# Palette weights as outer products of hat values on TensorE, two tile lags longer, and a new order of the pieces

## The chip, the cores and the metric

The kernel runs on one NeuronCore of a Trainium2 chip. The metric is the device time of one execution in microseconds, median of the runs. Five engines work from instruction streams of their own and meet only at semaphores: TensorE (PE, its weight loads are shown as PEld), VectorE (DVE), ScalarE (ACT), GpSimd (POOL) and SyncE (SP, which issues DMAs).

## The reference, cut to what matters

Eight residual layers follow each other over 2,048 tokens of 128 features: a recurrent attention with a clipped 8x8 state, a mixture of experts (first kind), the palette layer, the same mixture again, linear attention, a mixture of experts (second kind), a decayed recurrent attention, and the second mixture again. The change is at the palette layer. For each token it picks 15 earlier tokens, runs a small network over their relations, and gets for each pick k a point (gx, gy) and a mixing weight. It then reads a 16x16 picture (the palette, 128 channels) at the 15 points by bilinear interpolation and sums:

```
z = jnp.tanh(h @ Wc + bc)
w = jnp.nan_to_num(jax.nn.softmax(mix, axis=-1))
fx = jnp.clip((gx + 1.0) * 0.5 * (PW - 1), 0.0, PW - 1)
fy = jnp.clip((gy + 1.0) * 0.5 * (PH - 1), 0.0, PH - 1)
...
samples = ((1 - wy) * (1 - wx))[..., None] * g(y0, x0) + ((1 - wy) * wx)[..., None] * g(y0, x1) + ...
V = jnp.einsum('btkd,btk->btd', samples, w[:, 0])
y = jnp.einsum('btd,dm->btm', V, Wo[0])
```

The four bilinear factors are products of two "hats", relu(1 - |fx - x|) over the 16 columns x and relu(1 - |fy - y|) over the 16 rows y. So each token needs a 16x16 matrix of weights, the sum over k of w_k hat(fy_k, y) hat(fx_k, x), and then a product of these 256 weights with palette times Wo.

## The kernel before, in words

The tokens are 16 tiles of 128. Twelve stages pass over them, each written as a generator that yields between pieces: `front` (f), `gram` (g) and `scan` (s) with `out` (o) are the first attention, `ffn2` (a) and `ffn4` (b) the first mixture, `pal` (p) and `mix` (m) the palette layer, `lin` (l) linear attention, `ffn6` (c) and `ffn8` (e) the second mixture, `dec` (d) the decayed attention. For each engine a string, `ORDER`, says stage by stage by one letter whose next piece comes; the instructions of an engine stand in that order and are executed in it. Tiles of different stages so overlap like a pipeline. The scan of the first attention is a strict chain over the 2,048 tokens in pairs (64 steps a tile on DVE: L916 product, L924 scan), helped by small matmuls on PE, L539 and L549.

`ffn2` and `ffn4` share buffers and one count of uses; `LAG = 2` says by how many tiles the uses of `ffn4` stand behind those of `ffn2`. `ffn6` and `ffn8` share likewise, and alternate without a lag (uses 2c and 2c + 1).

The piece in question, `mix`, goes for a tile like this. After the small network (PE L674 to L696), DVE adds a bias, ACT takes tanh and exp, DVE scales and clips the coordinates (L1123, L1126) and makes the weights (L1129, L1131). POOL subtracts the grid (L1693, 30 x 16 values per token), ACT makes |.| and relu (L1462, L1465), and POOL multiplies the y hats by the weights (L1698). Then 8 times: POOL makes the products of the hats of two picks with tokens on partitions (`pr`, 128x512, L1705), and PE transposes and sums them in PSUM by matmuls with `pr` as weights and the identity as moving operand (L704, four or two of 128x128, each of two passes as all f32 matmuls here). ACT copies the sum (L1469), two matmuls multiply it by `palWo` (L712, L713) and DVE adds it to the residual (L855).

Each layer norm has on DVE statistics (L841, L843), the addition of eps (L845) and the normalisation (L849), and between the last two a power on POOL (L1573).

Of the kernel before, what the change touches and what calls it, by code (L numbers as in the profile page):

```python
# [99 lines left out]
LN_V, LN_G, LN_A, LN_P = ["bs", "ba", "le", "xn"], ["lr"], ["xt"], ["T"]  # L100
# [8 lines left out]
        "ssfffggffgsgsfssgsfsfsgsssssssgssssssssgssssssfssgsossosoosofssfsgsosossasaasssgsasaasasasassspgspsssspsfspp"  # L109
        "ppsosgsoososossssgsssosossasaasssasaasasasasfgsfmsgpmsspmsmssmmpsfmpspmmmsompmgpsoosoomsmssmsmsgsososmmsmsam"  # L110
        "saassgsasaasmsasaasmsmfsmmspfsmspmsmgsmmmsmmbspbbsfosmpmpmsmmmmpmobobbspoobbbsgmsmlslmsmsgsssllollllsomsmmms"
        "slslsacsacsamccsmccccsmccamsaascmasaasdmdspfsmdddspmgmfddddbsmgbbesmsefsmeebseeebebeebbebsomspolsolsmosospsm"
        "pmmllllllsmmsmpmgpgfsfllsmsmcsmcsomoccmccccmccsmsamsaacssadaadsadddaammddsmsgddsmmspgespmesmseeeeeeeesmsfesm"
        "smmsombmbbsosoospobmmmsmbbpspmbbbsmmopmgsopfllsamsaasllllllsmsamgssaamlsalsamasmmsmcgcfsccccccsccsmcsmsmdspm"
        "dsmdddsmpmgmsddmddsmsmbmebbsfesmeeboeeebebesebbebsoosolsposmmmlspspmsmmmpmsgllllllsmmpgsomomlsfmlsmmsmfcsscs"
        "gccsmccccccsasmcsaasmmsdmdsadddsaammmmsddddsaasamesgmebsbbeespeeeeeespfbebbsombbbsoosolsolsmspgsllllllspmsmp"
# [1862 lines left out]
```

## Time and profile before

| | |
|---|---|
| median of 3 runs | 1754.71 us (1746.64 to 1755.44) |
| profiled execution | 1746.41 us, span 1744.3 us |
| granted TensorE clock, mean | 0.768 |
| busy: PE, DVE, POOL, ACT | 1376.0, 1242.0, 969.9, 702.4 us |
| HBM traffic | 15 GB/s over the span |

The span is from the first to the last instruction. Busy time of an engine is the time in which at least one of its instructions is shown as running. Granted clock 1.0 is 2.4 GHz, 0.5 is 1.2 GHz; there is nothing between them in this trace, so a mean of 0.768 is a mixture.

### The profile page before, as it was taken

The numbers are of one execution on the slowest core, as the hardware profiler recorded it, in microseconds if no ns is written. First come the engines' busy times: TensorE is split into PE (matmuls) and PEld (weight loads), VectorE is DVE, ScalarE is ACT, GpSimd is POOL, SyncE is SP. The second block draws the span as 40 slices with busy tenths as digits, with TensorE's granted clock in tenths as the row PEclk, the third lists the DMA queues.
The fourth block names the chain that finished last, engine by engine and source line by source line (L and its number), as shares of the span: only waits on it lengthen the run. The fifth ranks groups of instructions, "written<-read, shape, count | busy, mean of one in ns | idle before, by whom it ended". The sixth has DMA issues, their size and how long they took to land.

```text
span 1744.3 us, 42130 instructions
## 1 busy us (share of the span) xinstructions
PE 1376.0 (79%) x15708; PEld 951.5 (55%) x15708; DVE 1242.0 (71%) x5282; ACT 702.4 (40%) x1833; POOL 969.9 (56%) x1423
## 2 busy tenths in 40 slices
PE   2576887788988888788888898988889787867764
PEld 0233464556665655656575665656465655646543
DVE  3878778877877776778777788787778874534432
ACT  1222545453545445344526353553515243424221
POOL 2337667557575654766574757474564636362421
PEclk9555778888788688878878697768869686868865
DMA  5001000000000100000000100010010100000000
GB/s 139 1 1 29 19 13 24 6 19 14 12 21 5 27 3 19 15 18 11 19 14 5 27 5 26 6 27 3 4 27 5 27 5 22 10 20 6 1 2 4
DMA packets 24007, 28.93 MB, mean 17 GB/s; under 512 B 8953, under 2 KB 18842, under 8 KB 23794
## 3 DMA queue, kind: packets, MB, share of 16 engines
q0 software_dynamic: 8208, 16.57, 3.6%
q1 hardware_dynamic: 15586, 9.57, 1.9%
q8 instruction: 128, 2.10, 0.5%
q14 instruction: 85, 0.70, 0.1%
HBM read 24.71 MB, written 2.23 MB: 15 GB/s over the span
## 4 chain that ended last, share of the span: by engine, by line
PE 50%; DVE 28%; POOL 7%; ACT 7%; issue 6%; SPq 1%; DMA 0%; DVEq 0%; ACTq 0%; POOLq 0%
PE ps L704 5%; PE ps L626 4%; DVE sb L1187 4%; DVE ps L924 4%; PE ps L674 2%; PE ps L525 2%; DVE ps L916 2%; PE ps L651 2%; PE ps L767 2%; PE ps L806 2%; PE ps L760 2%; PE ps L539 2%; POOL sb L1684 2%; PE ps L607 2%; PE ps L814 2%
## 5 line engine op out<-in xcount | busy, mean ns | idle before, releaser
L924 DVE TENSOR_TENSOR_SCAN ps<-ps,sb 128x47 f32<-128x47 f32 (+3 forms) x1024 | 271.5, 265 | 35.1 <-DVE ps L916 0.5
L1684 POOL DMA_INDIRECT sb<-table,sb x240 | 235.9, 983 | 78.4 <-issue 54.5
L916 DVE TENSOR_TENSOR ps<-sb,ps 128x24 f32<-128x24 f32 (+3 forms) x1024 | 193.0, 188 | 13.2
L1573 POOL TENSOR_TENSOR sb<-sb 128x1 f32<-128x1 f32 x128 | 72.1, 563 | 169.3 <-DVE sb L845 168.6
L704 PE MATMUL ps<-sb 128*128 128x128 f32 x960 | 161.4, 322 | 2.1 <-POOL sb L1705 2.0
L1705 POOL TENSOR_TENSOR sb<-sb 128x512 f32<-128x512 f32 (+1 forms) x128 | 128.4, 1009 | 42.9 <-PE ps L704 41.2
L704 PEld LDWEIGHTS ps<-sb 128*128 128x128 f32 x960 | 142.3, 227 | 8.6 <-issue 3.2
L1250 ACT ACTIVATE sb<-ps 128x128 f32<-128x128 f32 x128 | 35.0, 276 | 212.2 <-PE ps L497 211.6
L855 DVE TENSOR_TENSOR sb<-ps,sb 128x128 f32<-128x128 f32 x128 | 36.8, 288 | 115.1 <-PE ps L781 59.4
L549 PEld LDWEIGHTS ps<-sb 32*32 32x32 f32 x2032 | 45.4, 116 | 119.2 <-issue 92.5
L539 PEld LDWEIGHTS ps<-sb 32*32 32x32 f32 x2032 | 44.2, 118 | 112.2 <-DVE sb L896 66.1
L539 PE MATMUL ps<-sb 32*32 32x32 f32 x2032 | 75.1, 223 | 33.8 <-DVE sb L896 33.0
L549 PE MATMUL ps<-sb 32*32 32x12 f32 x2032 | 68.1, 196 | 40.3 <-DVE sb L932 36.9
L525 PE MATMUL ps<-sb 128*128 128x480 f32 x128 | 87.3, 775 | 7.7 <-POOL sb L1594 2.4
L626 PE MATMUL ps<-sb 128*128 128x128 f32 x512 | 85.4, 325 | 0.0
L497 PE MATMUL ps<-sb 128*128 128x128 f32 x128 | 45.6, 360 | 49.7 <-DVE sb L849 46.4
L1165 DVE TENSOR_TENSOR sb<-sb,ps 128x512 f32<-128x512 f32 (+1 forms) x96 | 61.2, 640 | 28.3 <-ACT sb L1516 15.3
L1594 POOL TENSOR_TENSOR sb<-sb 128x480 f32<-128x480 f32 x64 | 64.7, 1022 | 27.1 <-ACT sb L1289 27.0
L626 PEld LDWEIGHTS ps<-sb 128*128 128x128 f32 x512 | 78.8, 237 | 0.7
L1439 ACT ACTIVATE sb<-ps 128x512 f32<-128x512 f32 x64 | 64.3, 1041 | 30.4 <-PE ps L663 30.4
L849 DVE TENSOR_SCALAR sb<-sb 128x128 f32<-128x128 f32 x128 | 58.1, 454 | 23.1 <-POOL sb L1573 22.7
L1756 POOL TENSOR_TENSOR sb<-sb 128x128 f32<-128x128 f32 x32 | 12.9, 403 | 110.8 <-ACT sb L1523 110.7
(300 smaller groups left out, 3725.8 us busy)
## 6 DMA issues: line engine op xcount, KB each, us to landing
sb<-table,sb POOLq DMA_INDIRECT x240
sb<-in_cs SPq DMA_DIRECT2D x16, 128.0 KB
sb<-in_x SPq DMA_DIRECT2D x4, 256.0 KB, 9.5
table<-sb SPq DMA_DIRECT2D x16, 64.0 KB, 1.8
sb<-dscr SPq DMA_DIRECT2D x64, 2.0 KB
out<-sb SPq DMA_DIRECT2D x16, 64.0 KB, 1.5
sb<-in_wex SPq DMA_DIRECT2D x1, 512.0 KB, 5.5
sb<-in_rvx SPq DMA_DIRECT2D x1, 512.0 KB, 4.6
```

Of the source, the lines that this page charges most:

```text
L525: e.matmul(b[:, 0:32 * LW], blk, g_.pp[j % 2][:, :], start=True, stop=True).then_inc(*g_.P("s"))
L539: x = e.matmul(psS[rows, 0:32], KZT[c % 2][rows, 32 * o1:32 * o1 + 32], R[g % 2][rows, :], start=g == 0, stop=True, skip_group_check=True)
L549: x = e.matmul(b[rows, 0:12], SB[g % 2][rows, :], KM[c2 % 2][rows, 4 * o2:4 * o2 + 4, :].rearrange("p a b -> p (a b)"), start=True, stop=True)
L626: x = e.matmul(b[:, 0:128], s.hw[j // 4][:, 128 * (j % 4):128 * (j % 4) + 128], wex[:, 128 * j:128 * j + 128], start=False, stop=j == 7)
L704: x = e.matmul(pb[:, 128 * h:128 * h + 128], p_.pr[k % 2][:, 256 * j + 128 * h:256 * j + 128 * h + 128], ident, start=(k == 0 and j == 0 a ...
L916: e.tensor_tensor(at(psP, p + ROW - 3 - 2 * m, [ROW, 3], [2, m], [1, 2]), AC[:, row(n, k), :, HIST - 2 * m:HIST].rearrange("p r (a b) -> p ...
L924: e.tensor_tensor_scan(at(psD, 16 + k + COMB * skip, [COMB, 3 * ROW - skip]), at(psP, p + skip, [1, 3 * ROW - skip]), Q[:, i % 32, skip:3 ...
L1187: e.tensor_tensor_scan(d_.pv[h][:, at], l[:, 128:256], d_.pv[h][:, at], cp[:, k:k + 1] if c % NT else 0.0, ALU.mult, ALU.add).then_inc(*d_ ...
L1573: e.tensor_tensor(st[:, 9:10], st[:, 8:9], mhalf[:, 0:1], ALU.pow).then_inc(*s.G("lr"))
L1594: e.tensor_tensor(g_.pp[j % 2][:, :].rearrange("p (a b c) -> p a b c", b=2, c=LW), at(KT[c % 3], 32 * j, [2, 16], [0, 2], [1, LW]), km[:, ...
L1684: e.indirect_dma_start(GA[:, k, :], None, table[0:128 * i + 129, :], bass.IndirectOffsetOnAxis(u[:, k:k + 1], 0)).then_inc(*p_.gat("gat"))
L1705: e.tensor_tensor(p_.pr[k % 2][:, 0:256 * m].rearrange("p (k y x) -> p k y x", y=16, x=16), hats[:, 1, 2 * k:2 * k + m, :].unsqueeze(3).to ...
```

## The change

For the palette's weights the products of hats move from POOL to PE. The coordinates and exponentials are transposed in 32x32 blocks on DVE (`e.transpose`), so that picks lie on partitions 32q to 32q + 14 for the 32 tokens of block q, 16 hat values to a token lie in a row. One matmul for each token then gives its 16x16 matrix: the y hats of 15 picks as weights, the x hats moving, 15 rows deep. Four such (q = 0 to 3) use four different 32x32 parts of the array; there are 32 x 4 of them for a tile. The product with `palW` becomes 16 x 4 matmuls of 16 rows and 128 moving columns. The softmax's division moves to the final addition. `H1` and `H2` of the small network now lie in the buffer `PT`.

Further: eps, the q/k norm arithmetic of `front` and two small maxima move from DVE to POOL; negations on DVE are folded into ACT and into the reduction; `sT`, `one8` and `selb` are padded with zeros from 24 to 128 rows, so that the matmuls L616 and L767 use all rows; `LAG` goes from 2 to 3, and `ffn8` gets a lag of 1 behind `ffn6` (`LAG1 = 1`); the strings of `ORDER` are new for all five engines.

```diff
-LAG = 2
+LAG = 3
+LAG1 = 1
...
-LN_V, LN_G, LN_A, LN_P = ["bs", "ba", "le", "xn"], ["lr"], ["xt"], ["T"]
+LN_V, LN_G, LN_A, LN_P = ["bs", "ba", "xn"], ["le", "lr"], ["xt"], ["T"]
...
 ORDER = {
     "PE":
...
-        "mmmmllcmcmmccmccccmccmmcmmddbdddbbddddbbbebebbeeeeeeeellellllllllcccccccccccdddddddddeeeeeeeeeee",
+        "ccccceeddeeddeeedeeeeddddeeeeeeeeeee",
...
-    selb, one8, identb = sb([24, HU], BF16), sb([24, 8], BF16), sb([128, 128], BF16)
+    selb, one8, identb = sb([128, HU], BF16), sb([128, 8], BF16), sb([128, 128], BF16)
...
@@ PE, ffn0 @@
-                        x = e.matmul(b[:, 128 * j:128 * j + 128], one8[:, 4 * h + j:4 * h + j + 1].to_broadcast([24, 128]),
+                        x = e.matmul(b[:, 128 * j:128 * j + 128], one8[:, 4 * h + j:4 * h + j + 1].to_broadcast([128, 128]),
@@ PE, mix @@
-            for k in range(8):
-                yield
-                w.wait_ge(*m_.V.at("z", c))
-                w.wait_ge(*m_.G.at(f"pr{k}", c))
-                for h in range(2):
-                    for j in range(2 if k < 7 else 1):
-                        x = e.matmul(pb[:, 128 * h:128 * h + 128],
-                                     p_.pr[k % 2][:, 256 * j + 128 * h:256 * j + 128 * h + 128], ident,
-                                     start=(k == 0 and j == 0 and h == 0), stop=(2 * k + j == 14), skip_group_check=True)
-                x.then_inc(*m_.P(f"acc{k}"))
...
-            e.matmul(b[:, 0:128], p_.c[:, 0:128], palWo[:, 0:128], start=True, stop=False)
-            e.matmul(b[:, 0:128], p_.c[:, 128:256], palWo[:, 128:256], start=False, stop=True).then_inc(*m_.P("mm"))
+            for k in range(32):
+                if k % 4 == 0:
+                    yield
+                    w.wait_ge(*m_.G.at("u4", c))
+                for q in range(4):
+                    rows = slice(32 * q, 32 * q + 15)
+                    x = e.matmul(pb[32 * q:32 * q + 32, 16 * k:16 * k + 16], hats[rows, 512 + 16 * k:544 + 16 * k],
+                                 hats[rows, 16 * k:16 * k + 16], start=True, stop=True)
+            x.then_inc(*m_.P("op"))
+            for k in range(16):
+                if k % 4 == 0:
+                    yield
...
+                for q in range(4):
+                    rows = slice(32 * q, 32 * q + 16)
+                    x = e.matmul(b[32 * q:32 * q + 32, 0:128], WT[rows, k:512:16], palW[rows, 128 * k:128 * k + 128],
+                                 start=k == 0, stop=k == 15)
+            x.then_inc(*m_.P("mm"))
@@ DVE, norm and mix @@
-            w.wait_ge(*s.V.at("ba", c))
-            e.tensor_scalar(st[:, 8:9], st[:, 7:8], 1e-5, None, ALU.add).then_inc(*s.V("le"))
...
-            e.tensor_scalar(t[:, 112:142].rearrange("p (j k) -> p k j", j=2), z3[:, :, 0:2], 7.5, 7.5, ALU.mult,
-                            ALU.add).then_inc(*m_.V("f1"))
-            w.wait_ge(*m_.V.at("f1", c))
-            e.tensor_scalar(t[:, 112:142], t[:, 112:142], 15.0, 0.0, ALU.min, ALU.max).then_inc(*m_.V("f2"))
+            e.transpose(crdT[:, 0:64], crd[:, 0:64]).then_inc(*m_.V("xy"))
             yield
             w.wait_ge(*m_.A.at("ex", c))
+            e.transpose(crdT[:, 64:96], crd[:, 64:96]).then_inc(*m_.V("wt"))
...
-            e.tensor_scalar(t[:, 96:111], t[:, 66:81], t[:, 83:84], None, ALU.mult).then_inc(*m_.V("wk"))
-            yield from add(m_, m_.P.at("mm", c), ("pal", "mm", c), c, i)
+            e.scalar_tensor_tensor(out=X[:, i, :], in0=bk.of["pal", "mm", c][:, 0:128], scalar=t[:, 83:84], in1=X[:, i, :],
+                                   op0=ALU.mult, op1=ALU.add).then_inc(*m_.X("x"))
@@ ACT, mix @@
-            e.activation(hs, hs, ACT.Abs).then_inc(*m_.A("ab"))
+            e.activation(hats[:, 0:1024], hats[:, 0:1024], ACT.Abs, scale=7.5).then_inc(*m_.A("ab"))
...
-            e.activation(p_.c[:, :], pb[:, 0:256], ACT.Copy).then_inc(*m_.A("c"))
+            e.activation(WT[:, :], pb[:, :], ACT.Copy).then_inc(*m_.A("c"))
@@ POOL, norm and mix @@
+            w.wait_ge(*s.V.at("ba", c))
+            e.tensor_scalar(st[:, 8:9], st[:, 7:8], 1e-5, None, ALU.add).then_inc(*s.G("le"))
...
-                e.tensor_tensor(p_.pr[k % 2][:, 0:256 * m].rearrange("p (k y x) -> p k y x", y=16, x=16),
-                                hats[:, 1, 2 * k:2 * k + m, :].unsqueeze(3).to_broadcast([128, m, 16, 16]),
-                                hats[:, 0, 2 * k:2 * k + m, :].unsqueeze(2).to_broadcast([128, m, 16, 16]),
-                                ALU.mult).then_inc(*m_.G(f"pr{k}"))
+            hy = hats[:, 512:1024].rearrange("p (t y) -> p t y", y=16)
+            e.tensor_tensor(hy, hy, crdT[:, 64:96].unsqueeze(2).to_broadcast([128, 32, 16]), ALU.mult).then_inc(*m_.G("u4"))
```

Two places of PE's order show what the new strings do. The first is in the middle of the program, before the change: the last of the palette weights of one tile, L704, between pieces of `scan` (L549) and of a mixture of the second kind (L591 to L767).

```order
L704 MATMUL ps<-sb 128x128 x4
L549 MATMUL ps<-sb 32x12 x4
L704 MATMUL ps<-sb 128x128 x4
L591 MATMUL ps<-sb 24x128
L760 MATMUL ps<-sb 128x128 x4
L704 MATMUL ps<-sb 128x128 x2
L767 MATMUL ps<-sb 128x128 x4
L760 MATMUL ps<-sb 128x128 x4
L767 MATMUL ps<-sb 128x128 x4
```

The end of the same work of a tile after the change: L708 are the outer products, L720 the product with `palW`; L551 is the former L549, L541 the former L539, L823 the former L814, L619 the former L616, L787 to L790 the end of a mixture of the second kind (before: L778 to L781), L594 the former L591.

```order
L551 MATMUL ps<-sb 32x12 x4
L708 MATMUL ps<-sb 32x16 x64
L594 MATMUL ps<-sb 24x128
L619 MATMUL ps<-sb 128x128 x4
L787 MATMUL ps<-sb 128x128
L788 MATMUL ps<-sb 128x128
L790 MATMUL ps<-sb 128x128 x11
L619 MATMUL ps<-sb 128x128 x4
L823 MATMUL ps<-sb 128x128 x2
L541 MATMUL ps<-sb 32x32 x4
L823 MATMUL ps<-sb 128x128 x2
L720 MATMUL ps<-sb 32x128 x16
```

What moved: 30 matmuls of a full array in eight pieces have become 128 small ones in up to eight pieces and 64 small ones in up to four. (In such rows a count is of matmuls; in the trace each f32 matmul is two instructions.)

The second place is the end of the program before the change, the last tile's `dec` (L794 to L814) and the start of its `ffn8`.

```order
L796 MATMUL ps<-sb 32x128
L800 MATMUL ps<-sb 128x128
L806 MATMUL ps<-sb 128x128 x8
L814 MATMUL ps<-sb 128x128 x8
L497 MATMUL ps<-sb 128x128
L752 MATMUL ps<-sb 128x8
L591 MATMUL ps<-sb 24x128
L760 MATMUL ps<-sb 128x128 x4
```

And after it, the last tile's `dec` (L805, L809, L815) with what now stands between, the `ffn8` of the tile ahead of it (L594, L769, L776).

```order
L805 MATMUL ps<-sb 32x128
L594 MATMUL ps<-sb 24x128
L769 MATMUL ps<-sb 128x128 x4
L809 MATMUL ps<-sb 128x128
L815 MATMUL ps<-sb 128x128 x4
L776 MATMUL ps<-sb 128x128 x4
L769 MATMUL ps<-sb 128x128 x4
L776 MATMUL ps<-sb 128x128 x4
L815 MATMUL ps<-sb 128x128 x4
```

What moved: `ffn8` of a tile stands one tile later. Counted over PE's strings, what comes after the last piece of the scan was 3 tiles of `ffn4`, 4 of `lin`, `ffn6`, `dec` and `ffn8` each, and 2.7 of `mix`; it is now 4.1, 5, 5, 5, 6 and 2.9 tiles. At the end of the fifth tile of the scan, one tile of `lin`, `ffn6` and `dec` was done; now none is. Counted over the same rows, PE changes between different shapes of the array's part in use (all 128 x 128, or 32 rows, or 32 columns, or both) 1,488 times before and 1,301 times now.

## Rows read from the trace of the kernel before

**Rows 1.** The page's parts 1 and 4: busy time, chain by engine.

```profile
PE 1376.0 (79%) x15708; PEld 951.5 (55%) x15708; DVE 1242.0 (71%) x5282; ACT 702.4 (40%) x1833; POOL 969.9 (56%) x1423
...
PE 50%; DVE 28%; POOL 7%; ACT 7%; issue 6%; SPq 1%; DMA 0%; DVEq 0%; ACTq 0%; POOLq 0%
```

**Rows 2.** Scan steps L924 by stretch: us, DVE busy (count), clock, DMA share.

```profile
190.00:254.00 64.00, 16.75 (x63) 0.76 0.08 21
254.50:346.50 92.00, 16.95 (x64) 0.84 0.05 15
346.50:1432.70 1086.20, 186.17 (x704) 0.80 0.06 15
```

**Rows 3.** Windows: us, busy of PE, PEld, DVE, ACT, POOL, then clock.

```profile
1432.00:1744.30 312.30, 216.36 (x1897) 157.71 (x1895) 137.03 (x389) 100.18 (x243) 128.99 (x176) 0.71 0.03 9
346.00:1432.00 1086.00, 933.57 (x11134) 650.87 (x11132) 842.30 (x3607) 481.80 (x1255) 654.73 (x953) 0.80 0.06 15
```

**Rows 4.** PE's waits from 346 to 1432: us, times, longest.

```profile
PE ps L591 <- DVE sb L1014: 31.0, 22, 3.3
PE ps L497 <- DVE sb L849: 12.5, 17, 3.9
```

**Rows 5.** Groups by line, PE, what goes: busy us, mean ns.

```profile
L704 PE MATMUL ps<-sb 128*128 128x128 f32 x960 | 161.4, 322 | 2.1 <-POOL sb L1705 2.0
...
L712 PE MATMUL ps<-sb 128*128 128x128 f32 x32 | 8.3, 346 | 3.2 <-ACT sb L1469 3.2
...
L713 PE MATMUL ps<-sb 128*128 128x128 f32 x32 | 6.8, 296 | 0.0
```

**Rows 6.** Groups by line, PE, small matmuls (rows*columns of the array used).

```profile
L539 PE MATMUL ps<-sb 32*32 32x32 f32 x2032 | 75.1, 223 | 33.8 <-DVE sb L896 33.0
...
L674 PE MATMUL ps<-sb 128*32 128x16 f32 x4096 | 52.1, 190 | 10.5 <-issue 9.0 <-ACT sb L1439 1.5
```

**Rows 7.** PE in order of time near 795: start us, us, what.

```profile
794.93 1.16 PE L704 MATMUL ps<-sb 128*128 128x128 f32 x8
796.02 0.25 PE L549 MATMUL ps<-sb 32*32 32x12 f32 x8
796.20 1.16 PE L704 MATMUL ps<-sb 128*128 128x128 f32 x8
797.19 0.29 PE L497 MATMUL ps<-sb 128*128 128x128 f32 x1
...
798.92 0.26 PE L539 MATMUL ps<-sb 32*32 32x32 f32 x8
799.12 0.94 PE L626 MATMUL ps<-sb 128*128 128x128 f32 x6
```

**Rows 8.** The same near 786.

```profile
786.13 1.84 PE L704 MATMUL ps<-sb 128*128 128x128 f32 x8
787.90 0.39 PE L767 MATMUL ps<-sb 24*128 24x128 bf16 x4
```

**Rows 9.** Groups by line, DVE.

```profile
L896 DVE STREAM_TRANSPOSE sb<-ps 128x32 f32<-128x32 f32 x254 | 53.3, 210 | 0.0
...
L845 DVE TENSOR_SCALAR sb<-sb 128x1 f32<-128x1 f32 x128 | 19.6, 154 | 4.4
...
L1131 DVE TENSOR_SCALAR sb<-sb 128x15 f32<-128x15 f32 x16 | 7.2, 452 | 0.6
...
L870 DVE TENSOR_TENSOR sb<-sb 128x32 f32<-128x32 f32 x16 | 4.4, 278 | 0.5
```

**Rows 10.** Groups by line, POOL.

```profile
L1705 POOL TENSOR_TENSOR sb<-sb 128x512 f32<-128x512 f32 x112 | 118.2, 1062 | 31.0 <-PE ps L704 29.3
L1573 POOL TENSOR_TENSOR sb<-sb 128x1 f32<-128x1 f32 x128 | 72.1, 563 | 169.3 <-DVE sb L845 168.6
...
L1705 POOL TENSOR_TENSOR sb<-sb 128x256 f32<-128x256 f32 x16 | 10.2, 639 | 11.9 <-PE ps L704 11.9
...
L1742 POOL TENSOR_SCALAR sb<-sb 128x16 f32<-128x16 f32 x16 | 4.4, 278 | 4.8 <-DVE sb L1141 4.0
```

**Rows 11.** Groups by line, ACT.

```profile
L1465 ACT ACTIVATE sb<-sb 128x480 f32<-128x480 f32 x16 | 9.6, 599 | 0.3
```

**Rows 12.** The last tile's `ffn8` alone: the columns of rows 3.

```profile
1722.00:1738.00 16.00, 8.57 (x47) 5.53 (x47) 4.77 (x19) 4.60 (x12) 1.30 (x3) 0.50 0.02 6
```

More of the change, by code:

```diff
@@ L402, in _program @@
     PhT, GA = sb([128, T]), sb([128, 15, 128])
[L403 to L404 removed]
+    hats, crd, crdT, WT = sb([128, 1040]), sb([128, 96]), sb([128, 96]), sb([128, 512])
     p_.bb, p_.r, p_.h, p_.n, p_.it = sb([128, 512]), one([128, 256]), one([128, 256]), two([128, 16]), one([128, 128])
[L406 to L407 removed]
+    p_.u, p_.s, p_.csb, p_.z = two([128, 16], U32), two([128, 160]), one([128, 256]), sb([128, 48])
+    p_.rl = sb([128, 512])
+    p_.H1, p_.H2 = [[PT[:, x + 512 * p:x + 512 * p + 512] for p in range(2)] for x in (0, 1024)]
     table, dscr = t["table"], t["dscr"]
@@ L686, in mix @@
                 w.wait_ge(*m_.A.at(f"h{p}", c))
-                e.matmul(b[:, :], w2p[:, :], p_.H1[p][:, :], start=True, stop=True).then_inc(*m_.P(f"k{p}"))
-            hv = [p_.H2[p][:, :].rearrange("p (c k) -> p c k", k=16) for p in range(2)]
+                e.matmul(b[:, :], w2p[:, :], p_.H1[p], start=True, stop=True).then_inc(*m_.P(f"k{p}"))
+            hv = [p_.H2[p].rearrange("p (c k) -> p c k", k=16) for p in range(2)]
             for k in range(15):
@@ L816, in dec_ @@
             x.then_inc(*d_.P("mm"))
-        b = bank("prep", PA.at("pw", 0))
-        w.wait_ge(*loaded("pal"))
-        e.matmul(b[:, 0:128], pal[:, 0:128], wo2[:, :], start=True, stop=True)
-        e.matmul(b[:, 128:256], pal[:, 128:256], wo2[:, :], start=True, stop=True).then_inc(*PP("pw"))
+        for j in range(4):
+            b = bank(("prep", j), PA.at(f"pw{j}", 0))
+            w.wait_ge(*loaded("pal"))
+            for k in range(4 * j, 4 * j + 4):
+                for q in range(4):
+                    x = e.matmul(b[32 * q:32 * q + 32, 128 * (k % 4):128 * (k % 4) + 128],
+                                 PT[:, k:512:16], wo2[:, :], start=True, stop=True)
+            x.then_inc(*PP(f"pw{j}"))
         stages = {"front": front, "gram": gram, "scan": scan, "out": out, "ffn2": ffn0(a_, f2), "pal": pal_, "mix": mix,
@@ L1549, in dec_ @@
                          scale=0.5).then_inc(*d_.A("l"))
-        w.wait_ge(*PP.at("pw", 0))
-        e.activation(palWo[:, :], bk.of["prep"][:, 0:256], ACT.Copy).then_inc(*PA("pw"))
+        for j in range(4):
+            w.wait_ge(*PP.at(f"pw{j}", 0))
+            e.activation(palW[:, 512 * j:512 * j + 512], bk.of["prep", j][:, :], ACT.Copy).then_inc(*PA(f"pw{j}"))
         w.wait_ge(*loaded("dec"))
@@ L1794, in _ @@
         e.memset(zrow[:, :], 0.0).then_inc(*PG("zr"))
+        e.memset(hats[:, 1024:1040], 0.0).then_inc(*PG("zh"))
+        for k in range(2):
+            e.memset(a_.sT[k][:, :], 0.0).then_inc(*PG(f"z{k}"))
+        for k in range(2):
+            e.memset(b_.sT[k][:, :], 0.0).then_inc(*PG(f"z{2 + k}"))
         stages = {"front": front, "gram": gram, "out": out, "ffn2": ffn0(a_, f2), "pal": pal_, "mix": mix, "ffn4": ffn0(a_, f4),
```

352 lines of the change are left out of this document (177 added, 175 removed).

## The prediction

> **What bounds the kernel now.** I read the busy shares and the chain by engine first, then the pace of the scan, then windows, then waits. Busy time makes PE the fullest engine, 1376.0 of 1744.3 us, with DVE next at 1242.0; the chain that ended last lies for 50% on PE, for 28% on DVE and for 7% each on POOL and ACT [rows 1]. So there isn't one bound: the chain changes between the two fullest engines, and a microsecond taken from PE counts only where the chain is there. Over the whole kernel the scan sets the beat, because each of the 16 tiles has 64 of its steps. The fourth tile took 64 us, the fifth 92 us, and the next eleven 1086.2 us, so 98.7 us each [rows 2]. A scan of 64 steps can be had in 64 us, so in the steady part it isn't the scan's own chain that sets the 98.7 us, it is the work of the other stages between its steps. There PE is busy for 933.6 of 1086 us (86%) and DVE for 842.3 (78%). After the last step 312 us follow in which PE is busy for 216.4 (69%) and DVE for 137.0 (44%) [rows 3]. I call these parts fill (0 to 346), steady and tail. In the steady part the longest sum of PE's waits is for the expert pick: 31.0 us in 22 waits for DVE's L1014, and 12.5 us for the norm's L849 [rows 4].
>
> **PE, what goes.** L704 is 161.4 us of busy time, L712 and L713 are 8.3 and 6.8 us; together 176.5 us, 11.0 us a tile [rows 5].
>
> **PE, what comes.** The outer products are 32 x 4 matmuls a tile, each two instructions, 256, the same number and the same 16 moving columns as L674, whose 4096 instructions keep PE busy for 52.1 us [rows 6]. I take these 52 us. They differ in that four row parts are in use, as in L539: 2032 instructions in 75.1 us, 37 ns each, in isolated groups of eight with the wait of the pipeline in each [rows 6]. At that price 4096 would be 151 us; pieces of 32 to 128 instructions are nearer to L674 than to groups of eight, so 52 is the value and 151 the upper end.
>
> The product with `palW` is 16 x 4 matmuls of 128 columns, 128 instructions a tile. No row shows a 32-row matmul of 128 columns. What four parts of the array do at once must be read from the scan's groups of eight: L549 with 12 columns takes 0.18 us to the next start, L539 with 32 columns 0.20 us [rows 7]. L704 gives the price of a column: eight in 0.99 us (796.20 to 797.19) is 0.124 us for 128 columns, about 1 ns per column [rows 7]. One after the other, 20 more columns in each of eight matmuls would cost 0.16 us; they cost 0.02. So four go together. Then the new product has 32 turns a tile, each at L704's mean price, 161.4 / 960 = 0.168 us: 5.4 us a tile, 86 us in all. The upper end, none together, is 128 x 0.168 = 21.5 us a tile, 344 us; the lower end is 32 x 0.124 = 4.0 us a tile, 64 us.
>
> **PE, changes of shape.** L704 x8 followed by L549, another shape, takes 1.09 us to the next start; the same eight followed by L497, the same shape, 0.99 us [rows 7]. So a change costs 0.10 us here. The order has 1,488 of them before and 1,301 after, which takes off 187 x 0.10 = 19 us. I price the padding from 24 to 128 rows at nothing, since the columns that move stay the same.
>
> PE in sum: -176.5 + 52 + 86 - 19 = -57 us, -3.6 us a tile, 4.2% of its busy time. By the ends of the two unknown costs: from -79 to +300 us.
>
> **DVE.** L845 goes (128 times, 19.6 us), five operations of 32 columns in `front` (L870 is one of five, 4.4 us, so about 20 us), L1131 (7.2 us), and 96 small ones at 154 to 278 ns [rows 9], about 20 us: 67 us. The transposes come, 96 columns a tile, three times L896's 32 columns at 210 ns [rows 9], 10 us in all. Net -57 us, 4.6% of DVE.
>
> **POOL.** 128 instructions L1705 go, 118.2 + 10.2 = 128 us. Adding eps (128), `front`'s five (80) and 16 maxima come at L1742's 278 ns at most [rows 10], 62 us; three hat operations of 512 values instead of two of 480 and 240 add at L1705's 1.06 us about 25 us. Net -41 us. The norm now has two POOL operations behind each other where DVE did the first: 0.28 instead of 0.154 us, behind which the power L1573 stands anyway. POOL is idle 44% of the time, and DVE fills the wait with scan steps; I price it at nothing. Without that cover it would be 128 x 0.12 = 16 us.
>
> **ACT.** Two operations a tile grow from 480 to 1024 values, at L1465's 599 ns for 480 [rows 11] by 0.6 us each; with the wider copy 22 us on an engine that is busy for 40%: hidden. `H1` and `H2` in `PT` let the next tile's copies wait for this tile's last use of it; PE's order has the next tile's first transposes behind that use, so nothing is queued.
>
> **The sum.** Steady part: the two engines between which the chain changes lose 4.2% and 4.6%, so I take 4.2% off 98.7 us, 4.1 us a period, 45 us for eleven. The longer lag puts an independent tile's work before PE's wait for the pick; of those 31 us I take a third, 10 us. Fill: one tile of `lin`, `ffn6` and `dec` no longer stands within the fifth tile; its 92 us should come near the fourth's 64, -25 us. Tail: it gets one more tile of `lin`, `ffn6`, `dec` and `ffn4` and two of `ffn8`. A lone `ffn8` has 8.6 us of PE work [rows 12]; six stages at about 8 us are 48 us more PE work, less 3 x 3.6 us of `mix`. The tail has 96 us of idle PE, and the order puts an `ffn8` into the last `dec`, where PE had nothing; so I let most be absorbed and take +13 us (ends: 0 and +50).
>
> -45 - 10 - 25 + 13 = -67 us. The profiled execution took 1746.4 us, hence 1679 us. It lies 8 us under the median of the three; I add 6 for that: **1685 us**, 4% faster.
>
> **Rival 1: the four parts do not work together** at 128 columns. The L539 groups speak against it, but with short matmuls that hide behind the pipeline. It costs 258 us on PE: about 1940 us, slower. By the Trainium skill ("TensorEngine Tiling (Array Packing)", gotcha on PSUM pressure), different row tiles cannot access the same PSUM bank at one time, and here all four write one bank; by that rule this rival would come true. L539 and L549 write one bank from four row tiles as well, and the 0.02 us above is against it. 4%.
>
> **Rival 2: the outer products are late.** The first L708 waits for a line of POOL and ACT: two subtractions of 1.06 us, |.| and relu of 1.2 each, a product of 1.06, behind POOL's other work, 5.6 us at least; L704 needed only a first product before it began. If the order comes too early for them, PE stands, and with it the scan's matmuls queued behind, which DVE waits for. It turns the sign from 4.2 us a tile; at 6 us a tile 1685 + 96 = 1781 us, slower. For it: PE executes strictly in order. Against it: the new place was chosen with the longer line in it, and eight products of 1.06 us on POOL are gone. 8%.
>
> **Rival 3: the period stays.** If the steady part hangs on waits between engines rather than on their sums, only fill and tail change, -25 and +25: 1755 us, no change. Against it is PE's 86%. 7%.
>
> **Rival 4: the clock is lower.** The same L704 x8 took 1.77 us at 786.13 against 0.99 to 1.09 near 795 [rows 7, 8], which is 1.2 against 2.4 GHz; the mean in the steady part is 0.80, in the tail 0.71 [rows 3]. Full-array f32 work goes, 15- and 16-row work comes, and 24-row work becomes 128-row work, so it may go either way. At 0.76 in place of 0.80 PE's 934 us grow by 5%, 47 us: about 1732 us. 10%.
>
> **Rival 5: more than the sum.** PE idles for 368 us, and both lags and the new order aim there. A period of 92 us in place of 94 gives 25 us, a tail that stays at 312 another 13 us, the rest from `fill`: about 1640 us. 12%.
>
> **How the numbers follow.** The forecast has 59%. With rivals 4 and 5 the faster side (over 0.5%, about what a measurement here can tell from no change) has 80%, when a little is taken off for their edges; no change 8%, slower 12%. The forecast's own range is 1660 to 1715 us. The range reaches to rivals 5 and 4 and leaves out 1 to 3: 1630 to 1745 us.
>
> **What would show it.** Scan tiles 6 to 16 at 93 to 95 us each and the fifth near 70. L708 near 50 us and L720 near 86 us of PE busy time; rival 1 would show L720 above 200. DVE near 1185 us and POOL near 930. A tail of 320 to 330 us. Rival 2 would show a wait of L708 for POOL in PE's list, rival 4 a steady clock under 0.77. Wrong would be the forecast above all if the scan's period does not move.

## The result and the profile after

The changed kernel took 1665.06 us (median of 4 runs, 1649.73 to 1669.41) against 1753.28 us (4 runs, 1746.64 to 1755.44). The ratio is 0.9487, 95% interval 0.9419 to 0.9556: 5.1% faster, 20 us under the forecast of 1685 and inside its own range. The profiled execution took 1661.89 us. The steady part, the largest term of the sum that led there, came about in another way than the forecast says, as the experiments show.

Parts 1 and 4 of the page of after, which answer to [rows 1]:

```profile
PE 1346.5 (81%) x20952; PEld 941.7 (57%) x20952; DVE 1171.6 (71%) x4995; ACT 712.5 (43%) x1833; POOL 927.6 (56%) x1542
...
PE 56%; DVE 22%; ACT 8%; issue 7%; POOL 6%; SPq 1%; DMA 0%; DVEq 0%; ACTq 0%; POOLq 0%
```

POOL stands where it was forecast (930 us) and DVE 13 us under its forecast of 1185. PE lost 29.5 us, not 57, and a larger share of the chain lies on it than before.

Scan steps (L925, the former L924) by stretch, as in [rows 2]: tile 4, tile 5, tile 6, tiles 7 to 16.

```profile
191.20:254.80 63.60, 16.92 (x65) 0.63 0.08 21
254.80:317.70 62.90, 17.07 (x65) 0.72 0.08 22
317.70:394.50 76.80, 16.93 (x65) 0.81 0.07 18
394.50:1358.80 964.30, 168.66 (x641) 0.77 0.06 15
```

The fifth tile took 62.9 us where it took 92.0. The sixth is short too, because `ffn8` now begins a tile later. From the seventh on a tile takes 96.4 us; before, tiles 7 to 16 took 98.8 (443.9 to 1432.3 us, ten tiles). So of the 45 us that tiles 6 to 16 gained, 22 are the sixth tile's alone (98.3 before) and 24 are the other ten's.

Windows of after for fill, steady part and tail: us, busy of PE, PEld, DVE, ACT, POOL, clock, DMA. They answer to [rows 3].

```profile
0.00:318.00 318.00, 219.91 (x3210) 132.92 (x3211) 222.74 (x1148) 109.47 (x293) 170.14 (x308) 0.64 0.12 32
318.00:1358.70 1040.70, 894.60 (x14550) 635.63 (x14549) 786.33 (x3393) 481.61 (x1236) 623.81 (x1023) 0.77 0.06 16
1358.70:1660.00 301.30, 232.01 (x3202) 173.16 (x3195) 162.58 (x457) 121.45 (x305) 133.62 (x211) 0.78 0.04 11
```

The three parts gained 28, 45 and 11 us. The clock in the steady part fell from 0.80 to 0.77, and in the tail it rose from 0.71 to 0.78. The tail holds more work than before, 232 us of PE against 216, and is shorter.

Groups of PE by line, after: busy us, mean ns, idle before.

```profile
L629 PE MATMUL ps<-sb 128*128 128x128 f32 x512 | 100.1, 357 | 0.8 <-issue 0.8
L527 PE MATMUL ps<-sb 128*128 128x480 f32 x128 | 92.4, 819 | 4.1 <-POOL sb L1607 4.1
L720 PE MATMUL ps<-sb 16*32 16x128 f32 x2048 | 87.1, 335 | 0.0
...
L708 PE MATMUL ps<-sb 15*32 15x16 f32 x4096 | 63.3, 201 | 9.9 <-issue 9.2 <-POOL sb L1718 0.6
```

The two new products cost 150.4 us; 138 were forecast. But L629 and L527, which the change does not touch, grew from 85.4 to 100.1 and from 87.3 to 92.4 us (before they were L626 and L525). That is the clock: the same instructions ran more often at 1.2 GHz. Each start in the trace, set beside the granted clock of its moment, gives for the first of them 32% at 1.2 GHz before and 51% after, while the mean at a given level stayed the same (425 and 428 ns at 1.2 GHz, 279 and 281 at 2.4 for L626 and L629).

### The profile page after: what moved, and what is told of

It reads as the page before. It is cut to its first block, busy times and chain, and to the rows that moved or that the text cites. A ratio compares the mean times of both kernels' runs of the same rounds, so it can differ in the third digit from the quotient of the medians.

```text
span 1659.9 us, 52448 instructions
## 1 busy us (share of the span) xinstructions
PE 1346.5 (81%) x20952; PEld 941.7 (57%) x20952; DVE 1171.6 (71%) x4995; ACT 712.5 (43%) x1833; POOL 927.6 (56%) x1542
## 4 chain that ended last, share of the span: by engine, by line
PE 56%; DVE 22%; ACT 8%; issue 7%; POOL 6%; SPq 1%; DMA 0%; DVEq 0%; ACTq 0%; POOLq 0%
PE ps L629 5%; PE ps L720 4%; PE ps L527 3%; DVE ps L925 3%; PE ps L708 3%; PE ps L815 2%; PE ps L678 2%; DVE sb L1180 2%; DVE ps L917 2%; PE ps L541 2%; PE ps L823 2%; PE ps L610 2%; PE ps L551 2%; PE ps L568 2%; PE ps L654 2%
## 5 line engine op out<-in xcount | busy, mean ns | idle before, releaser
L925 DVE TENSOR_TENSOR_SCAN ps<-ps,sb 128x47 f32<-128x47 f32 (+3 forms) x1024 | 270.7, 264 | 38.6 <-DVE ps L917 0.5
L1571 POOL TENSOR_SCALAR sb<-sb 128x1 f32<-128x1 f32 x128 | 29.1, 227 | 165.1 <-DVE sb L856 162.7
L551 PEld LDWEIGHTS ps<-sb 32*32 32x32 f32 x2032 | 47.2, 119 | 115.9 <-issue 80.2
L541 PEld LDWEIGHTS ps<-sb 32*32 32x32 f32 x2032 | 45.4, 119 | 113.1 <-DVE sb L897 58.7
L629 PE MATMUL ps<-sb 128*128 128x128 f32 x512 | 100.1, 357 | 0.8 <-issue 0.8
L541 PE MATMUL ps<-sb 32*32 32x32 f32 x2032 | 75.0, 222 | 27.6 <-DVE sb L897 26.5
L551 PE MATMUL ps<-sb 32*32 32x12 f32 x2032 | 68.8, 197 | 35.2 <-DVE sb L933 28.7
L527 PE MATMUL ps<-sb 128*128 128x480 f32 x128 | 92.4, 819 | 4.1 <-POOL sb L1607 4.1
L866 DVE TENSOR_TENSOR sb<-ps,sb 128x128 f32<-128x128 f32 x112 | 31.8, 285 | 87.8 <-PE ps L790 36.0
L629 PEld LDWEIGHTS ps<-sb 128*128 128x128 f32 x512 | 90.2, 264 | 2.8 <-issue 1.6
L720 PE MATMUL ps<-sb 16*32 16x128 f32 x2048 | 87.1, 335 | 0.0
L933 DVE TENSOR_TENSOR sb<-ps,sb 128x32 f32<-128x32 f32 x254 | 45.8, 180 | 48.8 <-PE ps L541 47.8
L940 DVE TENSOR_TENSOR ps<-sb,ps 128x12 f32<-128x12 f32 x254 | 40.5, 160 | 51.8 <-PE ps L551 50.4
L720 PEld LDWEIGHTS ps<-sb 16*32 16x32 f32 x2048 | 71.5, 145 | 7.9 <-issue 1.9
L1615 POOL TENSOR_TENSOR sb<-sb 128x224 f32<-128x224 f32 x64 | 36.8, 574 | 65.5 <-ACT sb L1309 65.3
```

What stands on the lines that cost most here:

```text
L527: e.matmul(b[:, 0:32 * LW], blk, g_.pp[j % 2][:, :], start=True, stop=True).then_inc(*g_.P("s"))
L541: x = e.matmul(psS[rows, 0:32], KZT[c % 2][rows, 32 * o1:32 * o1 + 32], R[g % 2][rows, :], start=g == 0, stop=True, skip_group_check=True)
L551: x = e.matmul(b[rows, 0:12], SB[g % 2][rows, :], KM[c2 % 2][rows, 4 * o2:4 * o2 + 4, :].rearrange("p a b -> p (a b)"), start=True, stop=True)
L629: x = e.matmul(b[:, 0:128], s.hw[j // 4][:, 128 * (j % 4):128 * (j % 4) + 128], wex[:, 128 * j:128 * j + 128], start=False, stop=j == 7)
L720: x = e.matmul(b[32 * q:32 * q + 32, 0:128], WT[rows, k:512:16], palW[rows, 128 * k:128 * k + 128], start=k == 0, stop=k == 15)
L925: e.tensor_tensor_scan(at(psD, 16 + k + COMB * skip, [COMB, 3 * ROW - skip]), at(psP, p + skip, [1, 3 * ROW - skip]), Q[:, i % 32, skip:3 ...
```

## The experiments

Ratios are to the kernel before, timed together with the variants, with 95% intervals. Beside e1 to e7 and beside e12 its median was 1752 to 1753 us. e8 to e11 were timed together on another chip, and there it took 1825.37 us (11 runs); ratios and times of these four are compared only with each other. Theory A is that of the prediction: the gain follows the sum of engine work plus the shorter fill. Theory B is that work, order and clock act together.

**Which part of the change carries it.** e1 has the new palette work (with the padding) in the order and lags of before; e3 has all new instructions there.

```diff
-LAG = 3
-LAG1 = 1
+LAG = 2
+LAG1 = 0
...
 ORDER = {
```

(`ORDER` is that of before, with the products of POOL left out and PE's last pieces of `mix` split in four where one stood.)

> The new palette weights (outer products, H1 and H2 in PT, the folded negations, padding to 128 rows) in the order and with the lags of before: each last piece of mix on PE became four in the same place, the eight product pieces of POOL went. Eps and the arithmetic of front stay on DVE. Theory A (the gain is the sum of engine work, placed by the lags): PE loses 176 us and gets 150, plus 157 fewer changes of shape, 16 us, so about 40 us less PE work, 2.4%, and about 17 us less on DVE: 1725 us, ratio 0.98. Theory B (the gain is mostly a matter of the searched order fitting its work): the old order places the pieces where the old durations wanted them, so nothing is gained: ratio 1.00 or above.

Measured: 1807.23 us, 1.0278 (1.0226 to 1.0330), slower.

> All the new instructions, with eps and the arithmetic of front on POOL too, in the order and with the lags of before. Against e1 it has 40 us less DVE work. Theory A: another 10 to 15 us under e1, since the chain lies for a quarter to a third on DVE: ratio 0.97. Theory B: no difference to e1 beyond 0.5%. The distance from here to the changed kernel (0.949) is what lags and order give.

Measured: 1802.69 us, 1.0272 (1.0211 to 1.0333). The small operations moved to POOL bring nothing here.

e2 is the reverse: the work of before, unpadded, in the new order with lags 3 and 1 (`pr` pieces of POOL put where their inputs are first ready, and PE's four pieces of the last product made the one of before).

> The kernel before in the new order and with the new lags (3 and 1): four product pieces of mix on PE became the one of before, the pieces of POOL for the products of hats stand where they were first ready by their dependences. Theory A: fill gets 28 us shorter as in the changed kernel and the steady period stays at about 98 us, the tail at 301 to 325: 1725 us, ratio 0.98; together with e1 (0.98) that makes 0.96 of the 0.949. Theory B: old work in an order made for other work waits: ratio 1.00 or above. In either case the fifth scan tile should end near 318 us instead of 346, since that comes from the lags alone.

Measured: 1782.33 us, 1.0144 (1.0095 to 1.0192). Each half of the change alone is slower than the kernel before. e2's fill is 331.4 us long, where 318 was expected: the order and the lags give old work 15 of the 28 us. e2's list of PE's waits (us, times, longest):

```profile
PE ps L498 <- DVE sb L850: 45.9, 36, 7.4
PE ps L540 <- DVE sb L897: 42.5, 56, 2.2
PE ps L705 <- POOL sb L1704: 38.2, 37, 3.3
```

The products of POOL, for which PE waited 2.0 us before [rows 5], now hold it for 38.2 us. That is one loss of e2 and not the whole: PE's idle time grew by 20 us over all waits and its busy time by 22. These pieces of POOL also stand where a rule put them and not where a search did, so another placement might wait less. For e1 it is another thing. Its windows (fill, steady, tail):

```profile
0.00:361.70 361.70, 248.61 (x3443) 155.62 (x3443) 255.66 (x1274) 124.04 (x339) 176.49 (x291) 0.65 0.10 29
361.70:1486.10 1124.40, 958.48 (x14655) 679.68 (x14654) 816.07 (x3554) 493.77 (x1255) 587.00 (x888) 0.74 0.05 15
1486.10:1806.50 320.40, 212.47 (x2856) 159.37 (x2855) 130.36 (x377) 103.08 (x242) 109.68 (x156) 0.68 0.03 9
```

DVE and POOL have less to do than before in the steady part (816 and 587 us against 842 and 655), PE more, 958 against 934, at a clock of 0.74 against 0.80. Theory A, by which e1 should have gained, is refuted. PE's new work is less than the old and takes longer at the lower clock (the table behind e12).

e4 is the changed kernel with eps and the five operations of `front` back on DVE.

```diff
-LN_V, LN_G, LN_A, LN_P = ["bs", "ba", "xn"], ["le", "lr"], ["xt"], ["T"]
+LN_V, LN_G, LN_A, LN_P = ["bs", "ba", "le", "xn"], ["lr"], ["xt"], ["T"]
```

> The changed kernel with the 128 additions of eps and the five operations of front for each tile back on DVE, same order and lags. 40 us of DVE work come back (128 x 0.154 + 80 x 0.25). Theory A: the chain lies for 22% on DVE, so 9 to 20 us longer: ratio to before 0.955 to 0.96. Rival: DVE's 29% of idle time takes them, no change (0.949).

Measured: 1678.77 us, 0.9561 (0.9519 to 0.9604). The direction is that expected, 14 us, but the interval meets that of the changed kernel; their size stays open.

**Padding, price of the outer products, concurrency.** e5 takes the padding away.

```diff
-                sT = s.sT[c % 2][:, :]
+                sT = s.sT[c % 2][0:24, :]
...
-                        x = e.matmul(b[:, 128 * j:128 * j + 128], selb[:, at:at + 128], s.sT[c % 2][:, :], start=True,
+                        x = e.matmul(b[:, 128 * j:128 * j + 128], selb[0:24, at:at + 128], s.sT[c % 2][0:24, :], start=True,
```

> The changed kernel with the matmuls of the two expert stages back at 24 rows (sT, one8, selb cut to 24), same order and lags. The order then has 202 changes of shape more. Theory A (a change of shape costs 0.10 us on PE, the padding is otherwise free): 20 us more PE work, 15 to 20 us longer, ratio 0.96, and the busy time of the padded group L776 rises by its share. Rival (padding raises the clock): the granted clock falls by more than 0.02 and the time rises by 30 us or more. Rival 2: no change.

Measured: 1720.32 us, 0.9806 (0.9767 to 0.9846): 55 us of the 88 that the change gained go with it. Its windows:

```profile
0.00:318.10 318.10, 222.14 (x3194) 134.73 (x3195) 224.00 (x1145) 109.24 (x292) 170.37 (x308) 0.62 0.12 32
318.10:1403.20 1085.10, 949.20 (x14566) 663.40 (x14565) 786.99 (x3396) 482.40 (x1236) 624.03 (x1023) 0.73 0.06 15
1403.20:1716.60 313.40, 252.15 (x3195) 182.81 (x3195) 159.92 (x457) 122.09 (x305) 133.63 (x211) 0.71 0.04 10
```

Fill is as short as in after. The steady part takes 1085.1 us, what it took before (1086.2 [rows 2]), although DVE has 55 us less to do, and the tail 313.4 against 312.3 [rows 3]. Within the steady part the sixth scan tile and the ten behind it go different ways (L925: us, DVE busy, clock, DMA):

```profile
318.30:398.60 80.30, 16.92 (x64) 0.76 0.07 17
398.60:1403.20 1004.60, 168.46 (x641) 0.73 0.06 15
```

The sixth is 18 us shorter than before, and the others take 100.5 us each where they took 98.8. So without the padding the change gains where the lags act, in the fill and the sixth tile, and the period of the later tiles is no shorter. With the same order and nearly the same instructions PE's busy time in the steady part is 949 us instead of 895, at 0.73 instead of 0.77. The 202 changes of shape that come back would cost 20 us at the 0.10 us of [rows 7]; the table behind e12 leaves little room for more.

e6 issues the outer products twice.

```diff
-                for q in range(4):
+                for q in (0, 1, 2, 3, 0, 1, 2, 3):
```

> The changed kernel with each outer product (L708) issued twice, 4096 more instructions, same results. If four small matmuls go together also here, the price is that of L708 now, 63 us of PE busy time, and 50 to 65 us of time: ratio 0.98. If pieces hide in waits of PE (19% idle), 30 us or less: ratio 0.965.

Measured: 1766.09 us, 1.0049 (1.0017 to 1.0081), +101 us. The group of L708:

```profile
L708 PE MATMUL ps<-sb 15*32 15x16 f32 x8192 | 125.4, 206 | 50.7 <-issue 49.7 <-POOL sb L1718 0.9
```

Its busy time doubled, 62 us more, and its wait for issue grew from 9.2 to 49.7 us, 40.5 more. The two come to the 101 us, nearly: 4096 more of these tiny matmuls cost their own time and 40 us in which PE had none to run.

e7 puts the four k of one part of the array behind each other, where the changed kernel takes the four parts in turn.

```diff
-                for q in range(4):
-                    rows = slice(32 * q, 32 * q + 16)
...
+                if k % 4 == 0:
+                    for q in range(4):
+                        for kk in range(k, k + 4):
...
```

> The changed kernel with only the two inner loops of the product with palW exchanged: the four matmuls of one part of the array come one after the other, then those of the next part. Same instructions, same number, same results. If the parts work together only because neighbours in the queue are in different parts, L720 goes from 87 us towards 64 x 2 x 16 x 0.15 = 300 us and the time rises by 150 to 220 us (ratio 1.04 to 1.07). If the array takes a later matmul of another part ahead, nothing changes.

Measured: 1811.36 us, 1.0353 (1.0295 to 1.0411), +146 us. PE in order of time. First after, at 2.4 and at 1.2 GHz:

```profile
661.81 2.85 PE L720 MATMUL ps<-sb 16*32 16x128 f32 x96
1045.89 5.35 PE L720 MATMUL ps<-sb 16*32 16x128 f32 x96
```

Then e7, at 2.4 and at 1.2 GHz (the granted clock of the four stretches is 1.00, 0.50, 1.00 and 0.50):

```profile
1360.05 4.50 PE L722 MATMUL ps<-sb 16*32 16x128 f32 x64
914.55 11.45 PE L722 MATMUL ps<-sb 16*32 16x128 f32 x96
```

At 2.4 GHz that is 30 ns per instruction against 70, at 1.2 GHz 56 against 119: at the same clock the exchanged loops cost a factor of 2.1 to 2.4. A full-array instruction with as many columns took 124 ns at 2.4 GHz [rows 7], so e7 too has some overlap, and its 219.2 us stay below the 300 expected. e7's group by line:

```profile
L722 PE MATMUL ps<-sb 16*32 16x128 f32 x2048 | 219.2, 368 | 0.0
```

Four parts do work together at 128 columns, into one bank of PSUM (each to output partitions of its own), when neighbours in the queue use different parts: four instructions in the time of one of L704. The Trainium skill says otherwise ("TensorEngine Tiling (Array Packing)", Gotcha 1: different row tiles cannot access the same PSUM bank simultaneously); the 30 ns of after do not agree with it.

**Is it the rows?** e8 gives L708 and L720 32 rows instead of 15 and 16, the added ones zero on one side; e9 is e1 with that edit.

```diff
-                    rows = slice(32 * q, 32 * q + 15)
+                    rows = slice(32 * q, 32 * q + 32)
...
-                    rows = slice(32 * q, 32 * q + 16)
+                    rows = slice(32 * q, 32 * q + 32)
...
-        "pal": np.tile(b("palette").reshape(128, 256), (1, 2)), "wob": b("Wo")[0], "w1p": w1p, "w2p": w2p, "wcm": wcm,
+        "pal": np.pad(b("palette").reshape(128, 256), ((0, 0), (0, 256))), "wob": b("Wo")[0], "w1p": w1p, "w2p": w2p, "wcm": wcm,
```

> The changed kernel with the outer products (L708) 32 rows deep instead of 15 and the product with palW (L720) 32 rows deep instead of 16; the added rows are zeros on one side. Same instructions, same moving columns, same order, same number of changes of shape (1,301). Clock theory: the granted clock follows how many rows of the array are at work, as the step from 24 to 128 rows did (0.708 to 0.748); L708 had 31% of its instructions at the high level, L720 55%. Twice the rows there raise the clock, and the time falls by 0.5 to 2%, 1630 to 1657 us, with L708 and L720 themselves more often at the high level. Rival, changes of shape: what padding gave was 202 changes fewer, 0.27 us each; here none goes, so 1665 us within 0.5%. Rival, columns only: the same, no change.

Measured: 1757.30 us, 0.9658 (0.9605 to 0.9711). The changed kernel itself was not timed on this chip, so e8 can't be set beside it.

> The kernel of e1 (new palette work in the order and lags of before) with the same 32 rows in L707 and L719. e1 took 1807 us at a clock of 0.71, with PE busy for 1419.6 us. Clock theory: it is slow because the narrow work lowers the clock; with 32 rows the clock comes back to at least 0.73 and the time falls by over 1%, under 1790 us. Order theory: the pieces of the new work don't suit the place of the old ones (who waits for whom), and the clock follows from that; 1800 to 1810 us as e1.

Measured: 1839.19 us, 1.0113 (1.0063 to 1.0164), clock 0.737 in the profiled execution where e1 had 0.71. The times of the two are from different chips. Their traces can be compared line by line, since a matmul's duration at a given level is the same in both; first e1, then e9:

```profile
L719 PE MATMUL ps<-sb 16*32 16x128 f32 x2048 | 100.2, 379 | 4.4 <-ACT sb L1478 3.6 <-DVE sb L1191 0.8
```

```profile
L719 PE MATMUL ps<-sb 32*32 32x128 f32 x2048 | 67.8, 291 | 4.6 <-ACT sb L1478 4.4 <-issue 0.2
```

At 2.4 GHz an instruction of L719 takes 273 ns with 16 rows and 269 with 32, at 1.2 GHz 414 and 408. What changed is how many start at 2.4 GHz: 25% in e1, 84% in e9. The order is the same, and lines that the edit leaves alone stayed where they were (L628: 66% and 68%). The chips differ, but the lines left alone show no trace of that, so I take it that more rows in the same instructions raised the clock under them. For the outer products, L707, going from 15 to 32 rows changed nothing, 42% both times. Against e10, the padded kernel before on the same chip, e9 is still 4.1% slower, and its clock is 0.737 against 0.789. How much of that is the lower clock and how much the order's own waits is not separated.

e10 is the kernel before with the padding, and with the few instructions at the start that write the zeros.

```diff
-    selb, one8, identb = sb([24, HU], BF16), sb([24, 8], BF16), sb([128, 128], BF16)
+    selb, one8, identb = sb([128, HU], BF16), sb([128, 8], BF16), sb([128, 128], BF16)
...
```

> The kernel before with nothing but the padding: sT, one8 and selb with 128 rows, L617 and L768 using them all. Order and lags of before; 1,488 changes of shape become 1,283. Clock theory: more rows at work for 704 matmuls raise the mean clock from 0.768 by some 0.03, and the time falls by 1.5 to 3%, 1700 to 1727 us. Changes of shape at 0.27 us each (what e5 gave): -55 us, 1698 us; at the 0.10 us of rows 7: -20 us, 1733 us. If the padding paid only in the new order: 1753 us within 0.5%.

Measured: 1766.17 us, 0.972 (0.967 to 0.977), clock 0.781 to 0.794 in its six runs against 0.745 to 0.767 in the eleven of the kernel before beside it. So zeros in 104 rows of 608 matmuls (256 of L616 and 352 of L767; the 704 of the expectations counts too many) make the kernel before 2.8% faster by themselves. By e5 they are worth 3.3% in the changed one. On this chip e8 (1757.30 us), which has the whole change and more rows besides, lies only about half a percent under e10.

e11 pads the other short matmuls of the changed kernel: the two of the shared expert from 48 to 128 and the two with `cw1` and `cw2` of `dec` from 32 to 128. In each pair one grows in columns of the array and the other in rows.

```diff
-                e.matmul(b[0:48, 128:256], msu[:, 128:176], xt, start=True, stop=True).then_inc(*s.P("sh"))
+                e.matmul(b[:, 128:256], msu[:, 128:256], xt, start=True, stop=True).then_inc(*s.P("sh"))
...
-                e.matmul(b[:, 0:128], s.sh[0:48, 384:512], msd[0:48, 128:256], start=False, stop=False)
+                e.matmul(b[:, 0:128], s.sh[:, 384:512], msd[:, 128:256], start=False, stop=False)
...
```

> The changed kernel with the other short matmuls padded too: the shared expert's second half (L782, L788) from 48 to 128, dec's cw1 and cw2 (L805, L809) from 32 to 128; 1,301 changes of shape become 1,166, for 80 matmuls in all. Changes of shape at 0.27 us each: -36 us, 1629 us; at 0.10 us: -14 us, 1651 us. Clock theory by rows alone: 48 matmuls with more rows against the 704 of the first padding is 7% of its effect, under 5 us, 1660 to 1668 us.

Measured: 1756.87 us, 0.9669 (0.9607 to 0.9731). Like e8, it can't be set beside the changed kernel. Between the two, L720 was busy for 73.8 us in e8 (32 rows) and 82.0 in e11 (16 rows). What was different on that chip: PE's wait of L708 for issue, with times and longest, in after and in e8.

```profile
PE ps L708 <- issue: 9.2, 10, 2.1
```

```profile
PE ps L708 <- issue: 52.1, 81, 2.3
```

The same number of instructions, and PE stands for them 43 us longer. The profile does not show why they came later there.

**Both together.** e12 has the edits of e8 and e11.

> The edits of e8 and e11 together on the changed kernel: L708 and L720 32 rows deep, and the short matmuls of the shared expert and of dec padded to 128. In the call of e8 to e11 all kernels, the one before too, were some 4% longer than in the calls before it, and PE waited 102 us for issue in e8 and 101 in e11 against 35 us in the changed kernel's profile; so their ratios of 0.966 and 0.967 can't be set beside the 0.9487 of the changed kernel. If this call is again like the first ones (before near 1753 us): clock theory, more rows at work raise the clock above 0.748 and the ratio lies under 0.9487, at 0.925 to 0.942; rival, rows beyond the first padding bring nothing, 0.945 to 0.953; if the padding itself costs, above 0.956. If the call is like the last one (before near 1825 us), 0.955 to 0.967 whatever the theory, and the question stays open.

Measured: 1610.35 us (6 runs, 1598.29 to 1611.05), kernel before 1752.23 us (11 runs), ratio 0.9188 (0.9148 to 0.9229). This is 3.2% under the changed kernel by the ratios, and beyond what the clock theory had expected. The page of e12, part 1:

```profile
PE 1276.2 (79%) x20952; PEld 907.0 (56%) x20952; DVE 1170.3 (73%) x4995; ACT 711.4 (44%) x1833; POOL 928.7 (58%) x1542
```

Its windows for fill, steady part and tail:

```profile
0.00:311.00 311.00, 213.26 (x3206) 128.41 (x3207) 223.15 (x1144) 109.07 (x292) 170.18 (x308) 0.65 0.12 34
311.00:1322.40 1011.40, 852.30 (x14555) 615.32 (x14554) 784.91 (x3396) 481.02 (x1236) 624.87 (x1023) 0.81 0.06 16
1322.40:1608.80 286.40, 210.59 (x3194) 163.22 (x3193) 162.25 (x457) 121.31 (x305) 133.62 (x211) 0.81 0.04 11
```

And two of its groups:

```profile
L527 PE MATMUL ps<-sb 128*128 128x480 f32 x128 | 90.9, 806 | 4.1 <-POOL sb L1607 4.1
...
L720 PE MATMUL ps<-sb 32*32 32x128 f32 x2048 | 70.2, 288 | 0.5 <-issue 0.5
```

As many instructions as in after, the same order, the other engines the same to 2 us, and PE is busy for 70 us less at a mean clock of 0.78. Against after the steady part lost 29 us and the tail 15. L720 alone went from 87.1 to 70.2 us. The 135 changes of shape that went are 14 us at 0.10 us each; how the rest divides between the rows of L708 and L720 and the added padding, which e12 has together, stays open. Of the instructions of L720, 55% start at 2.4 GHz in after, 38% in e5 and 87% in e12.

**Busy time and clock together.** Busy time times mean clock is an estimate of what PE's work would take if all of it ran at 2.4 GHz (the mean is that of the whole span, not of the busy time alone). Profiled executions; idle is span minus busy.

| | PE busy, us | mean clock | busy times clock | PE idle, us |
|---|---|---|---|---|
| before | 1376.0 | 0.768 | 1057 | 368 |
| e10, before with padding | 1329.4 | 0.789 | 1049 | 434 |
| after | 1346.5 | 0.748 | 1007 | 313 |
| e5, after without padding | 1423.5 | 0.708 | 1008 | 293 |
| e1, new palette work, old order | 1419.6 | 0.710 | 1008 | 387 |
| e3, all new work, old order | 1393.1 | 0.726 | 1011 | 407 |
| e12, more rows and padding | 1276.2 | 0.780 | 995 | 333 |

The third column is nearly the same for all kernels with the same work, whatever their order and time. Between after and e5 it does not move, and the idle time is even shorter in e5, so the 77 us of busy time that the padding takes off go with the clock. A price of 0.27 us for each of the 202 changes of shape, which would also explain 55 us, has no place in these columns. e1 has 5% less work than the kernel before and is busy for 3% longer. The old order costs in a second way: e3 has the instructions of after and 93 us more idle time.

## Why the prediction was right, and where it wasn't

**The number** came out by parts that cancel: against the forecast the fill gained 3 us more, the steady part 10 us less and the tail 24 us more.

**The fill held.** -25 us forecast, -28 measured, the fifth tile at 62.9 us; e5 shows the same without the padding, so it is not the padding. e2 has the lags and the order with the old work and gets 15 us of it.

**The steady part came for another reason.** "... the two engines between which the chain changes lose 4.2% and 4.6%, so I take 4.2% off 98.7 us" is the step that failed. It takes the busy time for the work and so holds the clock constant. PE's work did shrink as forecast, by 4.7% in busy time times clock, and the clock fell with it: without the padding (e5) PE is busy for 1423.5 us at a clock of 0.708, the chain lies on it for 61%, and the steady part takes what it took before, the case of rival 3 (whose tail of +25 us has no row for what it is above the +13 of the sum). In sum I took 55 us off eleven periods and 45 came, and that is luck. The mean of tiles 6 to 16 is 94.6 us, inside my 93 to 95, but it is made of a sixth tile of 76.8, an effect of the lags that I had put into the fifth alone, and ten of 96.4, which by e5 would be 100.5 without the padding. The wait for the pick held: from 31.0 to 23.0 us in the steady part (L594 for L1015), 8 us where I took 10, and 24.0 in e5.

**"I price the padding from 24 to 128 rows at nothing, since the columns that move stay the same"** is the second failed step. By e5 it is worth 55 us, by e10 2.8% on the kernel before. The Trainium skill ("TensorE: Matmul & The Clock Gate", "Why this matters for your kernels") says that a single matmul 32 rows deep takes the time of one of 128. No run here compares these two depths in one line at one level; for 16 against 32 rows L719 agrees with it, 273 and 269 ns at 2.4 GHz. The gain came through the clock.

**Rival 4, the lower clock, is half true.** It named what would show it, a steady clock under 0.77, and at 0.77 after stands on its edge. Its two causes pull against each other. In e5, without the padding, it is 0.73 and the time 1720 us, near the 1732 that the rival gave; the padding brings it back. I had put both on one scale with a chance of 10% and no separate prices.

**The sizes on PE.** L720: 86 forecast, 87.1 measured. L708: 52 forecast, 63.3 measured, plus 9.9 us of idle time before it. That is near the 52 us of L674 and far from the 151 us of the upper end. PE in sum: -57 forecast, -29.5 measured. At the clock of before the work of after would keep PE busy for 1007 / 0.768 = 1311 us, an estimate: 65 us less. The lower clock gives 35 of these back, 20 of them on L629 and L527 alone, which the change doesn't touch.

**The tail went the other way.** +13 us forecast, -11 measured. The work came as counted (e5, at the clock of before, 0.71: 252 us of PE instead of 216), and e5's tail is 313.4 us long, the lower end of my bounds (0): all of it was absorbed. The other 12 us go with the clock, 0.78 instead of 0.71.

**Rival 1** (no concurrency) was wrong, and e7 shows what losing about half of the concurrency costs: 146 us with four of a part in a row. **Rival 2** (late outer products) did not come: L708 waits 0.6 us for POOL. **Rival 5** (more than the sum) came in part: the tail is shorter than its 312 us, the period of tiles 6 to 16 is not down to its 92.

**Additivity.** The forecast summed parts. New work in the old order is 2.7% slower even with the padding (e1, e3), old work in the new order 1.4% slower (e2), and both together without the padding 1.9% faster (e5). The order is fitted to its work; neither half has a price of its own. For the old work in the new order one wait is shown, that for POOL's products. For the new work in the old order the table shows 44 us more busy time at a lower clock and 19 us more idle time (e1 against before); why the clock is lower in that order stays open.

## What to carry to other kernels

Where matmuls use few rows of the array, pad them with zeros and read the granted clock: it cost no instruction of PE here, and brought 2.8% on the kernel before and 3.3% on the changed one; more of it, together with deeper palette matmuls, brought another 3.2%. A busy share doesn't tell how much work PE has, so read busy time and clock together. When parts of the array are to work together, let the innermost loop go over the parts. An order that was searched for one set of instructions has to be searched again for another, and the gain of work and order can't be added up from each alone.

## What the runs showed of the hardware

The granted clock went with how much of the array the matmuls fill, and not only with how much PE is busy: e5, after and e12 have the same order and 83%, 81% and 79% of busy time, and clocks of 0.708, 0.748 and 0.78. With 32 rows instead of 16, 84% of one line's instructions ran at 2.4 GHz instead of 25% (e9, e1). Which property of the added rows does it, the data being zeros, was not tested. Doubling 4096 tiny instructions cost 101 us, of which 40 are waits for issue. On one chip the same kernel took 4% longer (1825 against 1752 us), and in e8 there the small matmuls L708 waited five times as long for issue as in after; only runs that are timed together can be compared closely.
